# Both H transforms of the diagonal Fourier step as even and odd halves on 64x64 TensorE tiles, with GpSimd's additions and subtractions of rows 32 apart on either side

## The chip, the cores and the metric

One core of a Trainium2 chip runs the program; seven are idle. The metric is the device time of one execution in microseconds, the median of several runs.

## The reference

The input x has 8 images of 32 channels and 64x64 pixels. First comes one layer of content-dependent filtering (a 3x3 convolution to 16 channels, a leaky ReLU, a 1x1 convolution to nine logits, a softmax, and a 3x3 filter with these nine weights); the change leaves it alone. Then four layers of this, with h = 0.1:

```
Kj, Lj = project(K[j]), project(L[j])        # less their mean over the 3x3
z = relu(batchnorm(conv3x3(x, Kj)))
x = batchnorm(x + h * conv3x3T(z, Kj))
x = real(ifft2(fft2(x) * t)),  t = 1 / (h * |fft2(Lj)|^2 + 1)
```

batchnorm takes mean and variance over images and pixels, per channel. The last line is the Fourier step: a 2-d transform of every channel plane, a product with a real table, and the way back.

## The kernel before

**Layout.** An image pair (bp, four of them) has its channels and the row number modulo 4 on the 128 partitions, and 16 groups g of rows along the free side; X0 is the activation, Z0 the intermediate z, and X2, Z2 are the same moved by two rows, filled by DMA. A chunk c is a quarter of a pair, 4 groups, 512 columns, one PSUM bank; a layer has 16 chunks. All arithmetic is f32.

**Stages.** Per layer: `conv1` (16 chunks, 12 matmuls of 128x32 tiles each, into Z0), batchnorm and ReLU of z, `conv2` (16 chunks; VectorE adds 0.1 times each onto X0 at L864), the Fourier step per pair, and conv1 of the next layer. The Fourier step of a pair is a chain in which TensorE and VectorE take turns:

- `turn` (L879): VectorE transposes 32x32 blocks of X0 into one of three buffers `turned`.
- `fwdW` (L1113): 16 matmuls, the transform along W; VectorE transposes the four banks into `freqw` (L889).
- `slot0` and `fwdH` (L1123, L1129): the transform along H by one full 128x128 matmul a bank, four banks; VectorE multiplies with the table into `spec` (L912, L923). The frequency 0 of W holds two real columns and goes by itself: slot0, scaled, then slot0c (L1137), which ScalarE copies into `spec` (keep_slot0, L599).
- `invH` (L1146): the way back along H, a full matmul a bank; VectorE transposes into `backw` (L895).
- `invW` (L1160): 16 matmuls; VectorE transposes into `turned` again (move_back, L905), and ScalarE writes X0 from there with batchnorm's scale and bias (keep_invW, L614).

batchnorm's second use rides on the linearity of this: sums of X0 and of its square are taken by ScalarE behind each conv2 chunk (sum_x, L593), while the transform runs on unscaled data; the scale comes in at the end. Its chain is aggregate_x (L810 to L816), one small matmul (average, L1088), and scale_and_bias (L820 to L836). Behind it `prepare` (L657 to L665) makes the next layer's weights.

**What sets the order.** Each engine runs through the same list, layer_steps, and does its own part of each step, in that order. The eight PSUM banks are dealt out in the list's order: the step with number n has bank n % 8, and TensorE may start it once the last use of that bank has been read (Bank.claim). fwdW and invW start at a multiple of four. The buffers `turned` are used in rotation, 2 * bp + half modulo 3, on the way in and on the way back; move_back waits by x_back until the buffer's former content has been written to X0 (L904). SyncE copies X0 to X2 by DMA once half a pair is back (x_back), and conv1 waits for that.

## Time and profile before

| | |
|---|---|
| median of 3 runs | 695.63 us (694.91 to 696.49) |
| the profiled execution | 699.56 us, span 697.7 us |
| TensorE, matmuls | 643.2 us busy, 92% |
| VectorE | 487.7 us, 70% |
| ScalarE | 355.3 us, 51% |
| GpSimd | 95.5 us, 14% |
| TensorE's mean granted clock | 0.978 of full |

The span reaches from the first to the last instruction of the program; the execution's time has a little around it. The first 176 us are the filtering layer, in which GpSimd makes 80 of the products. A layer takes some 138 us behind it. The layers stand at 181.5, 319.0, 456.4 and 594.4 us (the first matmul of conv2). An engine's busy time is the union of its instructions; a matmul in f32 leaves two records, so that the counts of TensorE's rows are twice those of the code.

### The profile page before, as it was taken

The numbers are of one execution on the slowest core, as the hardware profiler recorded it, in microseconds if no ns is written. First come the engines' busy times: TensorE is split into PE (matmuls) and PEld (weight loads), VectorE is DVE, ScalarE is ACT, GpSimd is POOL, SyncE is SP. The second block draws the span as 40 slices with busy tenths as digits, with TensorE's granted clock in tenths as the row PEclk, the third lists the DMA queues.
The fourth block names the chain that finished last, engine by engine and source line by source line (L and its number), as shares of the span: only waits on it lengthen the run. The fifth ranks groups of instructions, "written<-read, shape, count | busy, mean of one in ns | idle before, by whom it ended". The sixth has DMA issues, their size and how long they took to land.

```text
span 697.7 us, 13525 instructions
## 1 busy us (share of the span) xinstructions
PE 643.2 (92%) x5392; PEld 221.3 (32%) x5392; DVE 487.7 (70%) x843; ACT 355.3 (51%) x672; POOL 95.5 (14%) x92
## 2 busy tenths in 40 slices
PE   6597999999999989999999899999998999999982
PEld 4222333222333333233333332333333323333330
DVE  3669888875886794638867946398679453886783
ACT  1454666663796223528961325299523152994233
POOL 0367666672000000000000000000000000000000
PEclk9689999999999999999999999999999999999996
DMA  9995111115800013583000226730003177100044
GB/s 187 183 171 91 32 32 33 31 31 127 190 2 1 1 28 97 131 176 102 1 1 1 52 72 156 155 99 1 1 1 79 46 176 154 40 1 1 1 105 137
DMA packets 44781, 51.10 MB, mean 73 GB/s; under 512 B 36528, under 2 KB 36656, under 8 KB 42672
## 3 DMA queue, kind: packets, MB, share of 16 engines
q1 hardware_dynamic: 40240, 48.95, 32.9%
q10 hardware_dynamic: 4480, 1.30, 1.2%
q8 instruction: 43, 0.70, 0.4%
q14 instruction: 18, 0.15, 0.1%
HBM read 11.96 MB, written 4.19 MB: 23 GB/s over the span
## 4 chain that ended last, share of the span: by engine, by line
PE 77%; DVE 15%; issue 3%; ACT 2%; DMA 1%; SPq 1%; POOL 0%; DVEq 0%; ACTq 0%; POOLq 0%
PE psum L978 48%; PE psum L1050 6%; PE psum L1146 5%; PE psum L1113 5%; PE psum L1129 3%; PE psum L1160 3%; PE psum L1001 3%; DVE work L923 2%; PE psum L1038 2%; DVE spare L895 1%; DVE work L889 1%; ACT Z L614 1%; DVE work L905 1%; DVE work L879 1%; PE psum L1080 1%
## 5 line engine op out<-in xcount | busy, mean ns | idle before, releaser
L978 PE MATMUL psum<-Z,wts 128*32 128x512 f32 x1536 | 168.2, 593 | 6.4 <-DVE Z L846 6.4
L978 PE MATMUL psum<-X,wts 128*32 128x512 f32 x1536 | 170.1, 593 | 0.6 <-issue 0.6
L593 ACT ACTIVATE work<-X,small 128x512 bf16<-128x512 f32 x128 | 90.7, 710 | 48.6 <-DVE X L864 48.6
L768 DVE BATCH_NORM_STATS2 stats<-Z 128x6 f32<-128x512 f32 x60 | 41.3, 692 | 79.3 <-ACT Z L508 79.2
L508 ACT ACTIVATE Z<-psum 128x512 f32<-128x512 f32 x64 | 38.2, 597 | 104.3 <-PE psum L978 93.2
L978 PEld LDWEIGHTS psum<-Z,wts 128*32 128x32 f32 x1536 | 51.6, 109 | 121.5 <-issue 108.5
L978 PEld LDWEIGHTS psum<-X,wts 128*32 128x32 f32 x1536 | 47.9, 109 | 111.7 <-issue 110.7
L571 ACT ACTIVATE Z<-Z,small 128x512 f32<-128x512 f32 (+4 forms) x92 | 80.2, 922 | 5.2 <-DVE small L836 4.7
L864 DVE SCALAR_TENSOR_TENSOR X<-psum,X 128x512 f32<-128x512 f32 x64 | 43.6, 690 | 39.0 <-PE psum L978 38.8
L1146 PE MATMUL psum<-work,cstS 128*128 128x512 f32 x128 | 59.2, 605 | 4.7 <-DVE work L889 3.9
L1129 PE MATMUL psum<-work,cstS 128*128 128x496 f32 x128 | 56.3, 582 | 0.0
L889 DVE STREAM_TRANSPOSE work<-psum 128x512 f32<-128x512 f32 x64 | 40.0, 680 | 16.6 <-PE psum L1113 16.6
L614 ACT ACTIVATE X<-work,small 128x512 f32<-128x512 f32 x36 | 28.7, 875 | 39.2 <-DVE work L905 39.2
L757 DVE TENSOR_TENSOR work<-Z,psum 128x512 f32<-128x512 f32 x52 | 33.6, 680 | 19.3 <-PE psum L1038 19.2
L923 DVE TENSOR_TENSOR work<-psum,tabT 128x496 f32<-128x496 f32 x64 | 39.6, 664 | 2.3 <-PE psum L1129 1.9
L1050 PE MATMUL psum<-work,cstS 128*32 128x512 f32 x168 | 36.2, 628 | 2.9 <-DVE spare L757 2.7
L1146 PEld LDWEIGHTS psum<-work,cstS 128*128 128x128 f32 x128 | 23.0, 189 | 40.6 <-issue 33.1
L757 DVE TENSOR_TENSOR spare<-Z,psum 128x512 f32<-128x512 f32 x48 | 30.9, 679 | 4.8 <-PE psum L1038 4.6
L1113 PE MATMUL psum<-work,cstS 32*64 32x512 f32 x384 | 31.4, 599 | 2.6 <-DVE work L923 2.6
L879 DVE STREAM_TRANSPOSE work<-X 128x512 f32<-128x512 f32 x48 | 32.1, 716 | 0.5
L905 DVE STREAM_TRANSPOSE work<-psum 128x1024 f32<-128x1024 f32 x24 | 28.8, 1225 | 5.1 <-PE psum L1160 5.1
L492 ACT ACTIVATE work<-psum 128x512 f32<-128x512 f32 x53 | 30.6, 595 | 2.9 <-ACT X L498 1.2
(122 smaller groups left out, 772.7 us busy)
## 6 DMA issues: line engine op xcount, KB each, us to landing
X<-X SPq DMA_DIRECT2D x64, 260.0 KB, 4.0
Z<-Z SPq DMA_DIRECT2D x32, 520.0 KB, 8.0
Z<-x SPq DMA_DIRECT2D x36, 128.0 KB, 4.2
out<-Z SPq DMA_DIRECT2D x24, 128.0 KB, 2.2
parS<-par SPq DMA_DIRECT2D x4, 673.0 KB, 8.6
Z<-x SPq DMA_DIRECT2D x12, 120.0 KB, 5.3
Z<-x ACTq DMA_DIRECT2D x14, 64.0 KB, 4.4
Z<-x SPq DMA_DIRECT2D x14, 64.0 KB, 4.7
```

The costliest lines, as they stand in the source:

```text
L571: last = nc.scalar.activation(z, z, ACT.Relu, bias=small[p0:p1, 13:14], scale=small[p0:p1, 12:13])
L593: nc.scalar.activation(by_row(rest[:, o:o + N // 2].bitcast(bf16)), xc, what, bias=small[:, 26:27], accum_out=sums[:, NCH * i + c:NCH * i ...
L757: nc.vector.tensor_tensor(by_line(product(c, dj, r)), around(c, dj, r), by_line(bank(n)), op=ALU.mult)\
L768: nc.vector.bn_stats(stats[:, 6 * c:6 * c + 6], rows(Z0, REG, c // Q, CH * (c % Q), CH))
L864: nc.vector.scalar_tensor_tensor(xc, in0=by_row(bank(n)), scalar=STEP, in1=xc, op0=ALU.mult, op1=ALU.add).then_inc(drained[n % BANKS], 1)
L889: nc.vector.transpose(freqw[:, N * q:N * q + N], src).then_inc(rows_moved, 1)
L923: nc.vector.tensor_tensor(to, src, tt, op=ALU.mult).then_inc(drained[n % BANKS], 1)
L978: last = nc.tensor.matmul(out_b[C * r:C * r + C, :], weights[:, o:o + C], rows(src, reg, bp, g, CH, dj - 1), start=(dj == 0), stop=(dj == ...
L1050: last = nc.tensor.matmul(bank(n)[C * r:C * r + C, :], cm(C_STACK, C), product(c, dj, r), start=(dj == 0), stop=(dj == 2), tile_position=( ...
L1113: last = nc.tensor.matmul(bank(first + r)[64 * half:64 * half + 64, :], cstS[k, C_FW + 64 * hi:C_FW + 64 * hi + 64], src[:, hi], start=(hi ...
L1129: nc.tensor.matmul(bank(n)[:, 0:16 * (SL - 1)], cm(C_FH), freqw[:, N * q:N * q + N].rearrange("p (a s) -> p a s", s=SL)[:, :, 1:SL], start ...
L1146: nc.tensor.matmul(bank(n), cm(to), spec[:, N * q:N * q + N], start=True, stop=True).then_inc(filled[n % BANKS], 1)
```

## The change

The transform along 64 rows splits by the parity of the frequency: even frequencies need only x[r] + x[r+32], odd ones only x[r] - x[r+32]. So the 128x128 matrix of H (real and imaginary part times 64 rows) falls into two of 64x64.

- GpSimd makes sums and differences of rows 32 apart (groups 8 apart) from X0 into Z0 (mix_halves), once conv2 has left both chunks. The turn takes both halves of a pair at once, from Z0, so it stands behind conv2's fifth chunk of a pair's count, and the Fourier steps move one chunk back in the list.
- fwdH and invH go by two banks: four matmuls of 64x64 at the four corners of the array, each bank half even, half odd. In the last layer invH remains a full matmul and puts the halves together itself. slot0, slot0c and the tables follow the new order of partitions.
- On the way back (not in the last layer) ScalarE scales the even and the odd buffer in place, the bias with the even one alone, and GpSimd writes their sum and difference into the two halves of X0 (unmix_halves). move_back's wait becomes one for the whole pair that had the buffer.
- ScalarE's sums are taken of Z0: the sum of the sums, and the squares of sums and differences, three instructions for two chunks instead of four; aggregate_x has two instructions more.
- In the list, aggregate_x moves behind fwdH of pair 2, scale_and_bias behind fwdW of pair 3, and invH of pair 3 ahead of the next conv1.

```diff
     after = {
-        5: fourier(j, 0, "fwdW"),
-        9: fourier(j, 0, "fwdH") + fourier(j, 1, "fwdW"),
-        13: fourier(j, 0, "invH") + fourier(j, 1, "fwdH") + fourier(j, 2, "fwdW"),
-        15: fourier(j, 1, "invH") + fourier(j, 2, "fwdH"),
+        6: fourier(j, 0, "fwdW"),
+        10: fourier(j, 0, "fwdH") + fourier(j, 1, "fwdW"),
+        14: fourier(j, 0, "invH") + fourier(j, 1, "fwdH") + fourier(j, 2, "fwdW"),
     }
     for c in range(NCH):
-        steps += [("conv2", j, c), ("turn", j, c)] + after.get(c, [])
-    steps += [("norm", j, 2)] + fourier(j, 3, "fwdW") + fourier(j, 0, "invW") + fourier(j, 2, "invH")
-    steps += fourier(j, 1, "invW") + fourier(j, 3, "fwdH")
-    rest = {1: fourier(j, 3, "invH"), 3: fourier(j, 2, "invW"), 5: fourier(j, 3, "invW")}
+        steps.append(("conv2", j, c))
+        if c and c % Q == 0:
+            steps.append(("turn", j, c // Q - 1))
+        steps += after.get(c, [])
+    steps += fourier(j, 1, "invH") + [("turn", j, BP - 1)] + fourier(j, 2, "fwdH") + fourier(j, 3, "fwdW")
+    steps += [("norm", j, 2)] + fourier(j, 0, "invW") + fourier(j, 2, "invH") + fourier(j, 1, "invW") + fourier(j, 3, "fwdH")
+    steps += fourier(j, 3, "invH")
+    rest = {3: fourier(j, 2, "invW"), 5: fourier(j, 3, "invW")}
     for c in range(NCH):
         if j + 1 < DEPTH:
             steps.append(("conv1", j + 1, c))
...
                     clear_edges(c // Q)
+
+            def mix_halves(j, bp, i):
+
+                bk.result(NUMBER["conv2", j, bp * Q + 2 + i])
+                low, high = (rows(X0, REG, bp, CH * (2 * half + i), CH) for half in range(2))
+                for half, op in enumerate((ALU.add, ALU.subtract)):
+                    nc.gpsimd.tensor_tensor(rows(Z0, REG, bp, CH * (2 * half + i), CH), low, high, op=op)\
+                        .then_inc(halves_mixed, 1)
+
+            def unmix_halves(j, bp):
+
+                pool.wait_ge(parts_scaled, 2 * (BP * j + bp) + 2)
+                even, odd = (turned[(2 * bp + p) % 3].rearrange("p (g b w) -> p g b w", b=2, w=W) for p in range(2))
+                for half, op in enumerate((ALU.add, ALU.subtract)):
+                    dst = rows(X0, REG, bp, 2 * CH * half, 2 * CH).rearrange("p g (w b) -> p g b w", b=2)
+                    nc.gpsimd.tensor_tensor(dst, even, odd, op=op).then_inc(x_back, 2)
+
+            for j in range(DEPTH):
+                for bp in range(BP):
+                    for i in range(2):
+                        mix_halves(j, bp, i)
+                for bp in range(BP if j + 1 < DEPTH else 0):
+                    unmix_halves(j, bp)
 
         @block.scalar
         def _(act):
...
-            def sum_x(j, c):
-                if c == 0:
+            def sum_x(j, bp):
+                if bp == 0:
                     act.wait_ge(shift_ready, j + 1)
-                bk.result(NUMBER["conv2", j, c])
-                xc = rows(X0, REG, c // Q, CH * (c % Q), CH)
-                for i, what in enumerate((ACT.Identity, ACT.Square)):
-                    m = 2 * (NCH * j + c) + i
-                    o = 4 * N - N // 2 * (m % 3 + 1)
-                    if m > 2:
-                        act.wait_ge(x_summed, m - 2)
-                    nc.scalar.activation(by_row(rest[:, o:o + N // 2].bitcast(bf16)), xc, what, bias=small[:, 26:27],
-                                         accum_out=sums[:, NCH * i + c:NCH * i + c + 1]).then_inc(x_summed, 1)
+                for i in range(2):
+                    act.wait_ge(halves_mixed, Q * (BP * j + bp) + 2 * i + 2)
+                    for s, (half, what) in enumerate(((0, ACT.Identity), (0, ACT.Square), (1, ACT.Square))):
+                        m = 3 * (2 * (BP * j + bp) + i) + s
+                        o = 4 * N - N // 2 * (s + 1)
+                        if m > 2:
+                            act.wait_ge(x_summed, m - 2)
+                        src = rows(Z0, REG, bp, CH * (2 * half + i), CH)
+                        bias = {} if half else {"bias": small[:, 26:27]}
+                        nc.scalar.activation(by_row(rest[:, o:o + N // 2].bitcast(bf16)), src, what, **bias,
+                                             accum_out=sums[:, PAIRS * s + 2 * bp + i:PAIRS * s + 2 * bp + i + 1])\
+                            .then_inc(x_summed, 1)
 
...
                 act.wait_ge(rows_back, 2 * (BP * j + bp) + q // 2 + 1)
+                if j < DEPTH - 1:
+                    if q % 2 == 0:
+                        part = turned[c // 2 % 3]
+                        bias = {} if q else {"bias": small[:, 13:14]}
+                        nc.scalar.activation(part, part, ACT.Identity, scale=small[:, 12:13], **bias).then_inc(parts_scaled, 1)
+                    return
                 src = turned[c // 2 % 3][:, N * (q % 2):N * (q % 2) + N].rearrange("p (g b w) -> p g b w", b=2, w=W)
-                if j == DEPTH - 1:
-                    both = Z2[:, bp * REG2:bp * REG2 + 2 * G * W].rearrange("p (b l w) -> p l b w", b=2, w=W)
-                    dst = both[:, CH * q:CH * q + CH]
-                else:
-                    dst = rows(X0, REG, bp, CH * q, CH).rearrange("p g (w b) -> p g b w", b=2)
+                both = Z2[:, bp * REG2:bp * REG2 + 2 * G * W].rearrange("p (b l w) -> p l b w", b=2, w=W)
+                dst = both[:, CH * q:CH * q + CH]
                 nc.scalar.activation(dst, src, ACT.Identity, bias=small[:, 13:14],
                                      scale=small[:, 12:13]).then_inc(x_back, 1)
 
...
-                src = X0[:, o + 2:o + 2 + g * GROUP].rearrange("p (g i) -> p g i", i=GROUP)[:, :, 0:ROW]
+                    nc.vector.tensor_scalar(S(26), stats[:, 1:2], -2.0, None, ALU.mult).then_inc(shift_ready, 1)
+
+            def turn(j, bp, half):
+
+                dve.wait_ge(halves_mixed, Q * (BP * j + bp) + 3 + half)
+                k, g = 2 * bp + half, 2 * CH
+                o = bp * REG + g * GROUP * half
+                src = Z0[:, o + 2:o + 2 + g * GROUP].rearrange("p (g i) -> p g i", i=GROUP)[:, :, 0:ROW]
                 for b in range(2):
                     dst = turned[k % 3].rearrange("p (m b c) -> p b m c", b=2, c=C)
                     last = nc.vector.transpose(dst[:, b], src.rearrange("p g (e l b) -> p b g e l", e=2, b=2)[:, b])
...
                 if k > 2:
-                    dve.wait_ge(x_back, NCH * j + 2 * (k - 2))
+                    dve.wait_ge(x_back, NCH * j + (2 * (k - 2) if j == DEPTH - 1 else Q * ((k - 3) // 2 + 1)))
                 nc.vector.transpose(turned[k % 3].rearrange("p (m e l) -> p e m l", e=2, l=32),
                                     psum[:, b0:b0 + 2, :].rearrange("p e (c m) -> p e m c", c=C)).then_inc(rows_back, 1)
 
...
-                            turn(*at)
+                        for half in range(2):
+                            turn(*at, half)
                     elif what == "fwdW":
                         move_rows(*at)
+                        if at[1] == 3 * Q + 3:
+                            scale_and_bias(j, 2)
                         if at[1] == 3 * Q + 3 and j + 1 < DEPTH:
                             dve.wait_ge(bn_ready, 2 * j + 2)
...
-                        if at[1] == 2 * Q - 1:
-                            aggregate_x(j)
                     elif what == "invW" and at[1] % 2 == 0:
                         move_back(j, at[1] // Q, at[1] % Q // 2)
                     elif what == "slot0":
@@ -956,7 +994,7 @@
                     elif what == "fwdH":
                         scale_fwdH(*at)
                         if at[1] == 2 * Q + 3:
-                            scale_and_bias(j, 2)
+                            aggregate_x(j)
                     elif what == "conv1":
                         conv1_stats(*at)
...
+                t = taps[:, N * (i % 2):N * (i % 2) + N]
+                nc.tensor.matmul(bank(n)[:, 0:N // 2], cm(e), t[:, 0:N // 2], start=True, stop=True)
+                for p in range(2):
+                    last = nc.tensor.matmul(bank(n)[64 - 64 * p:128 - 64 * p, N // 2:N], cstS[:, e + 64 * p:e + 64 * p + 64],
+                                            t[:, N // 2:N], start=True, stop=True, tile_position=(0, 64 - 64 * p))
+                last.then_inc(filled[n % BANKS], 1)
 
             def average(j, which):
...
             def forward_h(j, c):
-                n, q = NUMBER["fwdH", j, c], c % Q
-                bk.claim(n)
-                nc.tensor.matmul(bank(n)[:, 0:16 * (SL - 1)], cm(C_FH),
-                                 freqw[:, N * q:N * q + N].rearrange("p (a s) -> p a s", s=SL)[:, :, 1:SL],
-                                 start=True, stop=True).then_inc(filled[n % BANKS], 1)
+                first, q = NUMBER["fwdH", j, c], c % Q
+                for x in range(2):
+                    bk.claim(first + x)
+                for x in range(2):
+                    for p in range(2):
+                        k, half = slice(64 * p, 64 * p + 64), 64 * (p ^ x)
+                        src = freqw[k, N * (q + x):N * (q + x) + N].rearrange("p (a s) -> p a s", s=SL)[:, :, 1:SL]
+                        last = nc.tensor.matmul(bank(first + x)[half:half + 64, 0:16 * (SL - 1)], cstS[k, C_FH:C_FH + 64], src,
+                                                start=True, stop=True, tile_position=(64 * p, half))
+                    last.then_inc(filled[(first + x) % BANKS], 1)
...
             def inverse_h(j, c):
-                n, (bp, q) = NUMBER["invH", j, c], divmod(c, Q)
-                bk.claim(n)
-                bk.result(NUMBER["fwdH", j, c])
+                first, (bp, q) = NUMBER["invH", j, c], divmod(c, Q)
+                for x in range(2):
+                    bk.claim(first + x)
+                for x in range(2):
+                    bk.result(NUMBER["fwdH", j, c + x])
                 bk.result(NUMBER["slot0c", j, bp])
-                to = C_IL if j == DEPTH - 1 else C_IH
-                nc.tensor.matmul(bank(n), cm(to), spec[:, N * q:N * q + N], start=True,
-                                 stop=True).then_inc(filled[n % BANKS], 1)
+                for x in range(2):
+                    src = spec[:, N * (q + x):N * (q + x) + N]
+                    if j == DEPTH - 1:
+                        last = nc.tensor.matmul(bank(first + x), cm((C_IL, C_IX)[x]), src, start=True, stop=True)
+                    for p in range(2 if j < DEPTH - 1 else 0):
+                        k, half = slice(64 * (p ^ x), 64 * (p ^ x) + 64), slice(64 * p, 64 * p + 64)
+                        last = nc.tensor.matmul(bank(first + x)[half], cstS[k, C_IH + 64 * x:C_IH + 64 * x + 64], src[k],
+                                                start=True, stop=True, tile_position=(64 * (p ^ x), 64 * p))
+                    last.then_inc(filled[(first + x) % BANKS], 1)
```

Three places show what moves. The first is VectorE behind conv2's last chunk of a layer. Before (L864 the addition, L879 the turn, L895 invH, L811 to L816 the statistics, L912 and L923 the scaling, L889 fwdW):

```order
L864 SCALAR_TENSOR_TENSOR X<-psum,X 128x4x128 x2
L879 STREAM_TRANSPOSE work<-X 128x16x32 x2
L895 STREAM_TRANSPOSE spare<-psum 128x8x2x32 x4
L811 TENSOR_REDUCE small<-sums 128x2
L812 TENSOR_SCALAR small<-small 128x1
L813 TENSOR_SCALAR small<-small 128x2
L814 SCALAR_TENSOR_TENSOR small<-small 128x1
L815 TENSOR_SCALAR small<-small 128x1
L816 TENSOR_SCALAR small<-cstS,small 128x4
L912 TENSOR_TENSOR work<-psum,tabT 128x64
L923 TENSOR_TENSOR work<-psum,tabT 128x16x31 x4
```

And now (the same instructions are L902, L917, L933, L847 to L854, L950 and L961, L927):

```order
L902 SCALAR_TENSOR_TENSOR X<-psum,X 128x4x128
L933 STREAM_TRANSPOSE spare<-psum 128x8x2x32 x4
L917 STREAM_TRANSPOSE work<-Z 128x16x32 x4
L950 TENSOR_TENSOR work<-psum,tabT 128x64
L961 TENSOR_TENSOR work<-psum,tabT 128x16x31 x4
L847 TENSOR_REDUCE small<-sums 128x1
L848 TENSOR_REDUCE small<-sums 128x1
L849 TENSOR_SCALAR small<-small 128x1
L850 TENSOR_SCALAR small<-small 128x1
L851 TENSOR_SCALAR small<-small 128x1
L852 SCALAR_TENSOR_TENSOR small<-small 128x1
L853 SCALAR_TENSOR_TENSOR small<-small 128x1
```

The turn behind the last chunk has grown from two transposes to four, it stands behind those of invH, and the statistics have gone behind the scaling.

The second place is VectorE from the next layer's weights to conv1's statistics. Before (L905 move_back, L768 conv1's statistics):

```order
L657 TENSOR_REDUCE ksum<-parS 128x64
L665 SCALAR_TENSOR_TENSOR wts<-ksum,cstS,parS 128x96 x4
L670 COPY small<-parS 128x2
L905 STREAM_TRANSPOSE work<-psum 128x2x16x32 x2
L895 STREAM_TRANSPOSE work<-psum 128x8x2x32 x4
L905 STREAM_TRANSPOSE third<-psum 128x2x16x32
L905 STREAM_TRANSPOSE work<-psum 128x2x16x32
L912 TENSOR_TENSOR work<-psum,tabT 128x64
L923 TENSOR_TENSOR work<-psum,tabT 128x16x31 x4
L768 BN_STATS stats<-Z 128x6 x2
L895 STREAM_TRANSPOSE spare<-psum 128x8x2x32 x4
```

And now (move_back is L943, conv1's statistics L804):

```order
L943 STREAM_TRANSPOSE work<-psum 128x2x16x32 x2
L933 STREAM_TRANSPOSE work<-psum 128x8x2x32 x4
L943 STREAM_TRANSPOSE third<-psum 128x2x16x32
L943 STREAM_TRANSPOSE work<-psum 128x2x16x32
L950 TENSOR_TENSOR work<-psum,tabT 128x64
L961 TENSOR_TENSOR work<-psum,tabT 128x16x31 x4
L933 STREAM_TRANSPOSE spare<-psum 128x8x2x32 x4
L804 BN_STATS stats<-Z 128x6 x4
```

The order is the same but for invH of pair 3, which now stands ahead of conv1. The second of the two single move_backs (pair 1, second half) is the one that now waits for GpSimd's whole unmix of pair 0.

The third place is TensorE behind conv2's last chunk, up to conv1. Before:

```order
L1146 MATMUL psum<-work,cstS 128x512 x4
L1123 MATMUL psum<-work,cstS 128x64
L1129 MATMUL psum<-work,cstS 128x496 x4
L1137 MATMUL psum<-work,cstS 128x64
L1088 MATMUL psum<-small,cstS 128x5
L1113 MATMUL psum<-work,cstS 64x512 x16
L1160 MATMUL psum<-work,cstS 32x512 x16
L1146 MATMUL psum<-work,cstS 128x512 x4
L1160 MATMUL psum<-spare,cstS 32x512 x16
L1123 MATMUL psum<-work,cstS 128x64
L1129 MATMUL psum<-work,cstS 128x496 x4
L1137 MATMUL psum<-work,cstS 128x64
```

And now (invH is L1212, slot0 L1170 and L1172, fwdH L1184, slot0c L1195, fwdW L1155, the small matmul L1130, invW L1227, conv1 L1016), from invW of pair 0 on:

```order
L1227 MATMUL psum<-work,cstS 32x512 x16
L1212 MATMUL psum<-work,cstS 64x512 x8
L1227 MATMUL psum<-spare,cstS 32x512 x16
L1170 MATMUL psum<-work,cstS 128x2x16
L1172 MATMUL psum<-work,cstS 64x2x16 x2
L1184 MATMUL psum<-work,cstS 64x496 x8
L1195 MATMUL psum<-work,cstS 64x2x16 x4
L1212 MATMUL psum<-work,cstS 64x512 x8
L1016 MATMUL psum<-X,wts 32x512 x48
```

Four full matmuls have become eight of 64x64, and the last invH stands ahead of conv1's first chunk instead of behind its second.

## Rows read from the trace of the kernel before

**Rows 1.** The page, part 1: busy time and share of the span.
```profile
PE 643.2 (92%) x5392; PEld 221.3 (32%) x5392; DVE 487.7 (70%) x843; ACT 355.3 (51%) x672; POOL 95.5 (14%) x92
```
**Rows 2.** Busy time by stretch: conv2, the tail, conv1 (layer 2).
```profile
core 0: us, PE busy (x) PEld busy (x) DVE busy (x) ACT busy (x) POOL busy (x), PEclk, DMA share, GB/s
456.40:515.40 59.00, 58.82 (x513) 20.32 (x513) 44.99 (x67) 42.58 (x87) 0.00 (x0) 1.00 0.07 20
515.40:539.60 24.20, 21.01 (x142) 9.01 (x138) 22.85 (x51) 8.25 (x15) 0.00 (x0) 1.00 0.20 47
539.60:588.90 49.30, 49.27 (x457) 14.88 (x457) 21.76 (x30) 15.24 (x25) 0.00 (x0) 1.00 0.57 130
```
**Rows 3.** Order of time on PE in layer 0: start us, us, engine, line.
```profile
209.52 0.47 PE L1123 MATMUL psum<-work,cstS 128*128 128x64 f32 x2
...
215.59 10.51 PE L978 MATMUL psum<-Z,wts 128*32 128x512 f32 x96
226.04 3.70 PE L1146 MATMUL psum<-work,cstS 128*128 128x512 f32 x8
229.57 0.38 PE L1123 MATMUL psum<-work,cstS 128*128 128x64 f32 x2
229.78 3.50 PE L1129 MATMUL psum<-work,cstS 128*128 128x496 f32 x8
233.12 0.33 PE L1137 MATMUL psum<-work,cstS 128*128 128x64 f32 x2
233.38 0.66 PE L1113 MATMUL psum<-work,cstS 32*64 32x512 f32 x4
...
235.29 5.36 PE L978 MATMUL psum<-Z,wts 128*32 128x512 f32 x48
```
**Rows 4.** Order of time behind conv2 in layer 2, and one window of it.
```profile
515.39 3.70 PE L1146 MATMUL psum<-work,cstS 128*128 128x512 f32 x8
...
516.25 1.31 DVE L879 STREAM_TRANSPOSE work<-X 128x512 f32<-128x512 f32 x2
...
520.98 2.40 DVE L923 TENSOR_TENSOR work<-psum,tabT 128x496 f32<-128x496 f32 x4
...
525.91 2.51 DVE L889 STREAM_TRANSPOSE work<-psum 128x512 f32<-128x512 f32 x4 [0.69 <-PE psum L1113]
...
530.48 2.38 DVE L905 STREAM_TRANSPOSE work<-psum 128x1024 f32<-128x1024 f32 x2
...
539.63 5.36 PE L978 MATMUL psum<-X,wts 128*32 128x512 f32 x48 [0.60 <-issue]
...
523.30:525.21 1.91, 1.58 (x32) 0.69 (x32) 1.57 (x11) 0.29 (x1) 0.00 (x0) 1.00 0.00 0
```
**Rows 5.** GpSimd's products in the prologue: duration ns min/median/max.
```profile
L446 POOL TENSOR_TENSOR work<-Z,work x21: 1172/1183/1448, 29.5 to 158.2; 128x512 f32<-128x512 f32 x21
```
**Rows 6.** ScalarE's instructions by shape: busy us, mean ns.
```profile
L571 ACT ACTIVATE Z<-Z,small 128x1024 f32<-128x1024 f32 x4 | 4.9, 1228 | 0.0
```
**Rows 7.** The tail of layer 1, same columns as rows 2.
```profile
378.00:401.60 23.60, 20.94 (x143) 9.02 (x139) 22.22 (x50) 7.65 (x14) 0.00 (x0) 1.00 0.18 45
```
**Rows 8.** DMA issues: KB each, median us to landing.
```profile
X<-X SPq DMA_DIRECT2D x64, 260.0 KB, 4.0
```
**Rows 9.** TensorE at rest and at work, and the granted clock (PEclk).
```profile
21.30 1.99 PE L1015 MATMUL psum<-w2S,work 128*128 128x72 f32 x8 [2.94 <-ACT work L462]
...
682.14 1.92 PE L1160 MATMUL psum<-spare,cstS 64*32 64x512 f32 x32
...
21.00:22.00 1.00, 0.70 (x3) 0.70 (x4) 0.00 (x0) 0.25 (x1) 0.00 (x0) 0.66 1.41 172
33.00:38.00 5.00, 5.00 (x24) 0.91 (x16) 2.79 (x6) 1.08 (x3) 0.17 (x1) 0.50 1.05 165
38.00:39.00 1.00, 1.00 (x16) 0.30 (x16) 0.39 (x1) 0.66 (x1) 0.72 (x1) 0.81 0.97 167
686.50:687.00 0.50, 0.00 (x0) 0.00 (x0) 0.50 (x1) 0.50 (x2) 0.00 (x0) 0.91 0.00 0
```

78 lines of the change are left out of this document (49 added, 29 removed).

## Prediction

> **What bounds the kernel now.** I read the page first: TensorE (PE) is busy for 92% of the span, VectorE (DVE) for 70%, GpSimd (POOL) for 14%, all of that in the prologue [rows 1]. A share is an average, so the stretches of a layer come next [rows 2]. In the stretch of conv2, PE is busy 58.82 us of 59.00 and DVE 44.99. From conv2's end to the next conv1, PE is busy 21.01 of 24.20 us and DVE 22.85. In conv1's stretch PE is busy 49.27 of 49.30. The clock is full in all three. So PE sets the pace except in the 24 us behind conv2 (I call them the tail), where DVE does. What follows is a sum over these stretches, layer by layer.
>
> **What TensorE gives up.** Four banks by full 128x128 tiles take 3.5 us of issue: invH runs from 226.04 to slot0 at 229.57, fwdH from 229.78 to slot0c at 233.12 [rows 3]. Tiles in different rows and columns of the array run beside each other already: the sixteen 32x64 matmuls of fwdW take 235.29 - 233.38 = 1.91 us for four banks [rows 3]. So four 64x64 tiles should fill two banks in the time of one: for four banks fwdH 3.34 -> 1.7 us, invH 3.53 -> 1.75. PE saves 1.65 us in each of 16 fwdH and 1.8 us in each of 12 invH (the last layer's stay full tiles), 48 us in all. The question is how much of it reaches the end.
>
> The Trainium skill (TensorEngine Tiling (Array Packing), Theoretical Speedup) gives up to 2x for a dimension of 64 or less. By it the 48 us would come off whole, which makes 648 us. The rows of the tail speak against it.
>
> **What DVE allows.** DVE reads every one of those banks, and its price stays: four scalings of fwdH 2.40 us, four transposes of fwdW 2.51 (invH's are alike), two of invW 2.38, two of the turn 1.31 [rows 4]. That is 0.6 us a bank against PE's new 0.43. And fwdW claims the four banks that slot0 and the first three of fwdH had, so PE waits for DVE's third scaling. Behind conv2 chunk 10 (now chunk 9): slot0 0.25 us, the first pair full at 1.3, DVE's third scaling done at 3.15, fwdW issued 3.35 to 5.3; before, 215.59 - 209.52 = 6.07 [rows 3]. Saved: 0.8. Behind chunk 14 (now 13): invH 1.75, DVE's four transposes 1.1 to 3.6, its scalings of slot0 and three banks to 5.6, fwdW 5.8 to 7.7; before, 235.29 - 226.04 = 9.25 [rows 3]. Saved: 1.55. In the last layer, with full invH, the second is 0.45.
>
> **What GpSimd adds.** mix_halves has the form of the prologue's products, 128x512 f32 from two SBUF operands, median 1.18 us [rows 5]. Per pair of images there are four, the last two started by conv2's fourth chunk and done 2.4 us later. The turn stands behind the next chunk's addition, 2.6 us later, so in the middle of a layer nobody waits. unmix_halves does two of 1024 elements, with an output in steps of two. No row shows that size. It can hardly be cheaper than one of 512, 1.18, nor dearer than twice the slowest one, 2 x 1.45 = 2.9 [rows 5]. I take 2.3, near twice the median.
>
> **The tail, step by step,** from t = 0, where PE is through with conv2 chunk 15 (515.39 in the rows). Now [rows 4]: addition, two transposes of the turn at 0.9, four of invH, statistics, scalings to 8.0, fwdW's transposes 10.5 to 13.0, weights to 15.1, invW's transposes to 17.5, conv1 at 24.2. DVE works almost without a gap.
> New: addition to 0.85; GpSimd's last mix 0.9 to 3.25; meanwhile invH 1's transposes 1.1 to 3.55 on DVE, then the turn, now four transposes (of both halves, since rows 32 apart come together only here), to 6.05; slot0 and four scalings to 8.55; aggregate_x, two instructions longer, to 9.8. PE has issued invH 1 and fwdH 2 by 3.65 and can issue fwdW 3 only behind the turn and the second scaling, at 7.6. fwdW's transposes run 9.9 to 12.4, scale and bias (1.9 us, a window of its own in the rows) to 14.25, weights to 16.4, move_back of pair 0 to 18.85: 1.35 us later than the 17.5 of now.
> Then the new wait. move_back of pair 1's second half writes the buffer of pair 0's first half, and now waits for the whole unmix of pair 0. ScalarE scales 1024 elements in place (1.23 us, the row of that size [rows 6]) twice, to 20.2, GpSimd twice 2.3, to 24.9. DVE is there at 22.4 and stands 2.5 us. Behind it in DVE's queue are the scalings of fwdH 3, to 28.7; on ScalarE keep_slot0 stands behind pair 1's scaling, 27.8. invH 3, now ahead of conv1, ends at 29.7, and conv1 starts at 29.8. Before, conv1 started at 24.2 (layer 2) or 23.6 (layers 0 and 1 [rows 7]) and gave 3.55 us to invH 3 later. Like for like, that is 27.8 and 27.1. The tail costs 2.0 in layer 2 and 2.7 in the others. The copy to X2 (4.0 us to landing [rows 8]) starts at 22.6 and is in time.
>
> **conv1's stretch.** Pairs 2 and 3 leave through ScalarE and GpSimd too. conv1 chunk 8 stands at t = 54.6; its input is unmixed at 48.6 and copied at 53.2. Chunk 12 has more room. Nothing is added; but the cover is 1.4 us, and a GpSimd slower by more would open it.
>
> **Sum at full clock.** Layers 0 and 1: -0.8 - 1.55 + 2.7 = +0.35 each. Layer 2: -0.35. Layer 3 has no unmix; its two places save 0.8 and 0.45, and its chain reaches invW 2 at 28.8 instead of 27.0 (longer turn, late fwdW), +1.8: +0.55. In all +0.9 us. At no cost: ScalarE's sums (96 instead of 128, off the chain), the tables (half of a bank as two tiles side by side, the same passes), the wider constants (loaded under the prologue's work).
>
> **The clock.** The walk opens idle stretches on PE that the kernel now lacks: 3.65 to 7.6 and 23.5 to 27.9, each with only slot0c's four tiny matmuls inside, besides two of about 3 us. In the prologue PE stood 2.94 us until 21.30, and in that microsecond the granted clock fell from 1.00; at the end PE stops at 684.06 and it falls at about 686.95 [rows 9]. So 2.9 us of rest sufficed twice. It came back at about 38.4, after PE had been busy for all of 33.0 to 38.0 at 0.50 [rows 9]: 5.4 us at half pace lose 2.7. A fall in the late gap costs about that; a fall in the early one also lengthens fwdW and invW on the chain by 1.9 each, in all about 6.5.
> The Trainium skill (TensorE: Matmul & The Clock Gate, HAM oscillation) warns of just such gaps between bursts. With it the sum is 701.9, without it 696.5. The rows decide for it: both gaps are longer than the two that brought the clock down.
> I take two falls of 2.7 over the tails, +5.4.
>
> **Numbers.** The profiled execution is 699.56 us with a span of 697.7; the median of the runs is 695.63, 3.9 lower. I put the change on the median: 695.63 + 0.9 + 5.4 = 701.9.
>
> **Rivals.**
> 1. The clock stays up: 696.5, give or take 1.5. For it: the slot0c matmuls inside both gaps. Against: the length of the gaps. Chance 0.13.
> 2. Faster: PE's gain comes out whole in conv2's stretch. It decides at fwdW's claim: if DVE's third scaling is done when PE arrives, the two places save 1.65 and 3.45 instead of 0.8 and 1.55, 2.75 more per layer, and 2.1 more in the last: 0.9 - 8.3 - 2.1 = -9.5, which makes 686.1. Half of that, with my walk too long by 1 us a tail, gives 688. For it: DVE has 14 idle us in that stretch [rows 2]. Against: they lie elsewhere than in these bursts. This is what is left of the 2x rule, whose whole I hold for below 0.02. Chance 0.27, with times from 684 to 694.
> 3. GpSimd is slower on the strided output. At the upper bound of 2.9, DVE's stand grows by 1.2 us in three tails, 705.5; if the steps doubled its time to 4.6, by 4.6 and more, since conv1's cover goes as well, 716. Chance 0.10.
> 4. The change doesn't do what it says: the 64x64 tiles run two by two, with nothing saved on PE. The two places keep their length and the tail adds the same: 704 to 709. Against: the fwdW row. Chance 0.05.
> The forecast has 0.45, from 698 to 709.
>
> About 0.2%, 1.4 us, is what a measurement of this kernel can tell from no change. Faster by more: 0.27. Within: 0.12 (most of rival 1). Slower by more: 0.61. The range 687 to 712 leaves out the far ends of rivals 2 and 3.
>
> **What would show it.** In the new profile: fwdH and invH of four banks at 1.7 us on PE; conv2's stretch near 56.7 us; conv1's start near 30 us behind conv2's end; the second move_back of pair 1 waiting for GpSimd some 2.5 us; GpSimd 2.3 us for 1024 elements; a granted clock below 1.00 in some of the tails. I am wrong if conv2's stretch falls below 55 us, if conv1 starts within 28 us, or if the clock never leaves 1.00 in a layer.

## The result, and the profile after

The changed kernel took 713.44 us (median of 4 runs, 711.72 to 717.23) against 696.06 for the kernel before on the same chip (694.91 to 696.96): ratio 1.0258, 95% interval 1.0214 to 1.0302. It is 17 us slower, and 1.4 us beyond the upper end of the predicted range. The profiled execution took 713.42 us, with a span of 711.6 us; the mean granted clock went from 0.978 to 0.949.

The page after, busy time and the granted clock in 40 slices; the first answers to [rows 1]:

```profile
PE 627.1 (88%) x5840; PEld 205.7 (29%) x5840; DVE 494.9 (70%) x851; ACT 319.4 (45%) x584; POOL 232.8 (33%) x180
...
PEclk9699999999999988999999889999987999999996
```

TensorE (PE) was busy 16 us less, not 48: part of its work ran at half clock, and slot0 and the tables got dearer (below). The clock row shows where the clock fell: at the ends of layers 0, 1 and 2. The last layer has one short fall as well (676.7 to 680.2), too short for a digit; the 6 at the end stands behind the last matmul. By stretch in layer 2, with the columns of [rows 2]:

```profile
464.80:521.65 56.85, 54.78 (x560) 18.49 (x561) 42.99 (x65) 35.28 (x69) 17.65 (x14) 1.00 0.06 18
521.65:553.60 31.95, 22.86 (x210) 7.20 (x207) 26.28 (x58) 7.55 (x13) 10.81 (x6) 0.79 0.14 36
553.60:599.20 45.60, 45.60 (x452) 12.99 (x450) 22.68 (x27) 13.47 (x19) 10.58 (x5) 1.00 0.59 137
```

conv2's stretch is 2.15 us shorter. The tail is 7.75 longer, and 3.7 of that comes back in conv1's stretch, which no longer holds invH of pair 3. In the tail the granted clock is 0.79 where it was 1.00.

PE in conv2's stretch of layer 0, which answers to [rows 3] (slot0 L1170, fwdH L1184, conv2 L1016, invH L1212):

```profile
212.58 0.42 PE L1170 MATMUL psum<-work,cstS 128*128 128x32 f32 x2
...
218.17 10.51 PE L1016 MATMUL psum<-Z,wts 128*32 128x512 f32 x96
228.61 1.95 PE L1212 MATMUL psum<-work,cstS 64*64 64x512 f32 x16
230.49 0.41 PE L1170 MATMUL psum<-work,cstS 128*128 128x32 f32 x2
...
231.08 1.90 PE L1184 MATMUL psum<-work,cstS 64*64 64x496 f32 x16
232.79 0.37 PE L1195 MATMUL psum<-work,cstS 64*64 64x32 f32 x8
```

invH of four banks takes 230.49 - 228.61 = 1.88 us (it was 3.53), fwdH 232.79 - 231.08 = 1.71 (3.34). slot0, now in three pieces, takes 231.08 - 230.49 = 0.59 where it took 0.21 [rows 3]. The group behind chunk 10 takes 218.17 - 212.58 = 5.59.

The tail of layer 0 on PE answers to the PE rows of [rows 4]. t = 0 is 238.86, where PE is through with chunk 15; in brackets the idle time before and what ended it:

```profile
238.86 1.95 PE L1212 MATMUL psum<-work,cstS 64*64 64x512 f32 x16
...
245.12 0.42 PE L1195 MATMUL psum<-work,cstS 64*64 64x32 f32 x8 [1.90 <-DVE work L950]
246.28 3.43 PE L1155 MATMUL psum<-work,cstS 32*64 32x512 f32 x32 [0.74 <-DVE work L961]
...
253.14 3.41 PE L1227 MATMUL psum<-work,cstS 64*32 64x512 f32 x32 [2.92 <-DVE work L927]
...
266.96 0.51 PE L1195 MATMUL psum<-work,cstS 64*64 64x32 f32 x8 [2.85 <-DVE work L950]
268.26 3.69 PE L1212 MATMUL psum<-work,cstS 64*64 64x512 f32 x16 [0.79 <-ACT work L631]
271.88 3.36 PE L1016 MATMUL psum<-X,wts 128*32 128x512 f32 x20
```

Three groups run at half clock: fwdW 3 (3.43 us where 1.98 is normal), invW 0 (3.41 for 1.95) and invH 3 (3.69 for 1.88, with conv1's first chunk behind it). Each stands behind a gap. conv1 starts at t = 33.0; before, at 23.6 in this layer.

The wait that I had announced, on VectorE (DVE), and the GpSimd (POOL) instructions that it waited for:

```profile
261.64 1.25 DVE L943 STREAM_TRANSPOSE third<-psum 128x1024 f32<-128x1024 f32 x1
265.45 1.25 DVE L943 STREAM_TRANSPOSE work<-psum 128x1024 f32<-128x1024 f32 x1 [2.56 <-POOL X L471]
```

```profile
260.62 4.70 POOL L471 TENSOR_TENSOR X<-work 128x1024 f32<-128x1024 f32 x2 [18.33 <-ACT work L644]
```

And from the groups of the page (idle before them at the end):

```profile
L462 POOL TENSOR_TENSOR Z<-X 128x512 f32<-128x512 f32 x64 | 80.7, 1285 | 251.0 <-DVE X L902 251.0
...
L471 POOL TENSOR_TENSOR X<-work 128x1024 f32<-128x1024 f32 x12 | 28.3, 2383 | 60.7 <-ACT work L644 60.7
```

Last, a stretch that I had booked at nothing: from conv1's end to conv2. Before, and after (the tables are L1080, then L1119 and L1121):

```profile
175.94 1.98 PE L1080 MATMUL psum<-work,cstS 128*128 128x512 f32 x4
...
181.57 1.92 PE L978 MATMUL psum<-Z,wts 128*32 128x512 f32 x16 [1.58 <-DVE Z L846]
```

```profile
175.83 0.70 PE L1119 MATMUL psum<-work,cstS 128*128 128x256 f32 x2
176.46 0.65 PE L1121 MATMUL psum<-work,cstS 128*64 128x256 f32 x4
177.04 0.70 PE L1119 MATMUL psum<-work,cstS 128*128 128x256 f32 x2
...
182.05 1.50 PE L1016 MATMUL psum<-Z,wts 128*32 128x512 f32 x12 [1.08 <-DVE Z L884]
```

A table of two pieces now takes 177.04 - 175.83 = 1.21 us where it took about 0.95, and the stretch is 6.22 us long instead of 5.63. The four tables cost 1.04 us more; PE's wait ahead of conv2, 1.08 instead of 1.58, takes back 0.5 of it, and 0.6 is left.

**The span's balance** (711.6 - 697.7 = +13.9): tables 4 x 0.6 = +2.4; conv2's stretches -2.2 three times and -0.75 in the last; tail and conv1 together +6.6, +4.5, +4.1, and from conv2's end to the end of layer 3 +3.8, which is +19.0; the part ahead of the tables of layer 0 -0.1.

The medians lie 17.4 apart, 3.5 more than the two spans: the profiled execution of the kernel before is 3.5 us above its median, the one of the change is on it. What the layers' rows show of the change is 14 us; where the rest stands, no row shows. The part ahead of the first conv1, which the change leaves alone, takes up to 4 us more or less from one execution to another (last section), so below, a difference of medians stands beside what the profiles show from the first conv1 on.

### The profile page after: what moved, and what is told of

It is laid out like the page before. It is cut to its first block, busy times and chain, and to the rows that moved or that the text cites. A ratio compares the mean times of both kernels' runs of the same rounds, so it can differ in the third digit from the quotient of the medians.

```text
span 711.6 us, 14466 instructions
## 1 busy us (share of the span) xinstructions
PE 627.1 (88%) x5840; PEld 205.7 (29%) x5840; DVE 494.9 (70%) x851; ACT 319.4 (45%) x584; POOL 232.8 (33%) x180
## 4 chain that ended last, share of the span: by engine, by line
PE 72%; DVE 16%; ACT 4%; issue 3%; POOL 2%; DMA 1%; SPq 1%; DVEq 0%; ACTq 0%; POOLq 0%
PE psum L1016 46%; PE psum L1088 6%; PE psum L1155 5%; DVE work L961 3%; PE psum L1227 3%; PE psum L1039 3%; PE psum L1212 2%; PE psum L1209 2%; POOL X L471 2%; PE psum L1076 2%; DVE work L927 1%; DVE work L917 1%; ACT work L644 1%; ACT Z L649 1%; DVE work L943 1%
## 5 line engine op out<-in xcount | busy, mean ns | idle before, releaser
L1016 PE MATMUL psum<-Z,wts 128*32 128x512 f32 x1536 | 168.2, 593 | 4.3 <-DVE Z L884 4.3
L1016 PE MATMUL psum<-X,wts 128*32 128x512 f32 x1536 | 171.2, 598 | 0.1
L462 POOL TENSOR_TENSOR Z<-X 128x512 f32<-128x512 f32 x64 | 80.7, 1285 | 251.0 <-DVE X L902 251.0
L804 DVE BATCH_NORM_STATS2 stats<-Z 128x6 f32<-128x512 f32 x60 | 40.9, 691 | 68.4 <-ACT Z L537 68.0
L1016 PEld LDWEIGHTS psum<-Z,wts 128*32 128x32 f32 x1536 | 52.4, 109 | 117.1 <-issue 108.9
L1016 PEld LDWEIGHTS psum<-X,wts 128*32 128x32 f32 x1536 | 47.4, 110 | 117.9 <-issue 116.6
L624 ACT ACTIVATE work<-Z,small 128x512 bf16<-128x512 f32 x64 | 45.5, 712 | 53.9 <-POOL Z L462 53.9
L902 DVE SCALAR_TENSOR_TENSOR X<-psum,X 128x512 f32<-128x512 f32 x64 | 43.3, 676 | 36.1 <-PE psum L1016 36.0
L927 DVE STREAM_TRANSPOSE work<-psum 128x512 f32<-128x512 f32 x64 | 39.9, 683 | 18.2 <-PE psum L1155 18.2
L471 POOL TENSOR_TENSOR X<-work 128x1024 f32<-128x1024 f32 x12 | 28.3, 2383 | 60.7 <-ACT work L644 60.7
L961 DVE TENSOR_TENSOR work<-psum,tabT 128x496 f32<-128x496 f32 x64 | 38.5, 659 | 3.3 <-PE psum L1184 3.3
L943 DVE STREAM_TRANSPOSE work<-psum 128x1024 f32<-128x1024 f32 x24 | 29.3, 1236 | 15.5 <-POOL X L471 8.3
L1155 PE MATMUL psum<-work,cstS 32*64 32x512 f32 x384 | 33.7, 651 | 7.2 <-DVE work L961 7.2
L644 ACT ACTIVATE work<-work,small 128x1024 f32<-128x1024 f32 x18 | 21.2, 1193 | 38.6 <-DVE work L943 38.6
L452 POOL TENSOR_TENSOR tabT<-Z,work 128x512 f32<-128x512 f32 x21 | 24.7, 1189 | 26.6 <-PE psum L1088 26.6
L1212 PE MATMUL psum<-work,cstS 64*64 64x512 f32 x192 | 29.4, 735 | 2.3 <-ACT work L631 2.3
```

Source lines behind the costliest of these rows:

```text
L462: nc.gpsimd.tensor_tensor(rows(Z0, REG, bp, CH * (2 * half + i), CH), low, high, op=op)\
L471: nc.gpsimd.tensor_tensor(dst, even, odd, op=op).then_inc(x_back, 2)
L624: nc.scalar.activation(by_row(rest[:, o:o + N // 2].bitcast(bf16)), src, what, **bias, accum_out=sums[:, PAIRS * s + 2 * bp + i:PAIRS * s ...
L902: nc.vector.scalar_tensor_tensor(xc, in0=by_row(bank(n)), scalar=STEP, in1=xc, op0=ALU.mult, op1=ALU.add).then_inc(drained[n % BANKS], 1)
L927: nc.vector.transpose(freqw[:, N * q:N * q + N], src).then_inc(rows_moved, 1)
L961: nc.vector.tensor_tensor(to, src, tt, op=ALU.mult).then_inc(drained[n % BANKS], 1)
```

## The experiments

Three costs are candidates in the tail: the clock, DVE's wait for GpSimd, and the new place of invH 3. Each was taken away alone. Differences are to the median of the kernel before in the same series (696.59 us for the clock alone, DVE's wait alone, the place of invH 3 and the tables alone; 697.26 for the last two below; 697.10 for the other four; 19 to 23 runs each); the change itself stands at +17.4.

**The clock alone.** Full-size matmuls whose result nobody reads fill PE's gaps in the tail. The order of the work stays.

```diff
+            def filler(n, cols):
+                for m in cols:
+                    nc.tensor.matmul(bank(n)[:, 0:m], cm(C_AVG), cstS[:, 0:m], start=True, stop=True)
 ...
+                if bp == 2:
+                    filler(n, (512, 512) if j < DEPTH - 1 else (512,))
+                if bp == 3 and j < DEPTH - 1:
+                    filler(n, (512, 512, 512))
```

(with 512, 512 and 256 columns ahead of invW 0, and 256 ahead of invH 3, 512 in the last layer.)

> The changed kernel with full-size filler matmuls (their results are overwritten) on TensorE wherever it stands in a tail: 2 of 512 columns ahead of slot0c of pair 2, 2.5 ahead of invW of pair 0, 3 ahead of slot0c of pair 3, half a one ahead of invH of pair 3. By my theory the granted clock is half of what the tails cost: conv1 and the last transforms run at half pace after each gap, 9.7 us over the four tails beyond the walk at full clock. Then the clock stays at 1.00 in all layers and the time falls from 713.4 to 704, give or take 1.5. Rival: VectorE's queue and GpSimd alone make the tails long, and the low clock falls where TensorE waits anyway: 712 to 715 with the clock up.

Measured: 704.02 us (703.17 to 704.63), ratio 1.0101 (1.0065 to 1.0137), clock 0.975: +7.4. The tail of layer 0 on PE (t = 0 at 236.93; L1190 is the filler):

```profile
244.36 1.98 PE L1155 MATMUL psum<-work,cstS 32*64 32x512 f32 x32 [0.80 <-DVE work L961]
...
256.23 3.51 PE L1240 MATMUL psum<-spare,cstS 64*32 64x512 f32 x32 [2.60 <-DVE work L943]
...
266.06 1.95 PE L1222 MATMUL psum<-work,cstS 64*64 64x512 f32 x16
267.94 2.35 PE L1016 MATMUL psum<-X,wts 128*32 128x512 f32 x20
```

fwdW 3 and invH 3 are back at full clock, and conv1 starts at t = 31.0 instead of 33.0. The clock still falls once, ahead of invW 1 (3.51 us), here and in layer 1 (3.06). In layer 2 (t = 0 at 515.14) the same gap brings no fall, and conv1 starts at t = 29.8:

```profile
534.08 1.95 PE L1240 MATMUL psum<-spare,cstS 64*32 64x512 f32 x32 [2.58 <-DVE work L943]
...
544.95 10.52 PE L1016 MATMUL psum<-X,wts 128*32 128x512 f32 x96
```

By the medians the fillers give back 17.4 - 7.4 = 10.0 us. The two profiles, from the first conv1 to the end, give 8.3: 3.0, 1.5 and 2.3 from conv2's end to the next conv2, and 1.5 in the last layer. So the clock is 8 to 10 us of the cost.

**DVE's wait alone.** A fourth buffer for pair 1's second half, in the part of Z2 that is free then, so that move_back need not wait for pair 0's unmixing. No filler.

```diff
+        o4 = 3 * REG2 + GROUP
+        fourth = Z2[:, o4:o4 + 2 * N]
+
+        def back(j, k):
+            return fourth if k == 3 and j < DEPTH - 1 else turned[k % 3]
 ...
-                if k > 2:
+                if k > 2 and (j == DEPTH - 1 or k != 3):
```

> The changed kernel with a fourth buffer (free columns of Z2 of pair 3) for the second half of pair 1 on the way back, so that VectorE's move_back no longer waits for GpSimd's unmix of pair 0. Theory: this stand of 2.5 us is on the chain in three tails, so 7.5 us go, 706, and up to 5 more if the shorter gap keeps the clock up (701). Rival: the next wait ends at the same time (keep_slot0 behind ScalarE's scaling, or conv1 on the copy to X2), and the time stays above 711.

Measured: 699.93 us (698.0 to 704.07), ratio 1.0046 (1.0016 to 1.0076), clock 0.953: +3.3. Its tail in layer 0 (t = 0 at 238.99):

```profile
246.42 3.48 PE L1160 MATMUL psum<-work,cstS 32*64 32x512 f32 x32 [0.74 <-DVE work L966]
...
253.32 3.50 PE L1232 MATMUL psum<-work,cstS 64*32 64x512 f32 x32 [2.96 <-DVE work L932]
...
264.47 0.42 PE L1200 MATMUL psum<-work,cstS 64*64 64x32 f32 x8 [0.18 <-DVE work L955]
265.77 2.22 PE L1217 MATMUL psum<-work,cstS 64*64 64x512 f32 x16 [0.88 <-ACT work L636]
267.92 6.65 PE L1021 MATMUL psum<-X,wts 128*32 128x512 f32 x60
```

The gap ahead of slot0c is 0.18 us instead of 2.85, invH 3 is fast again, and conv1 starts at t = 28.9. The early falls (fwdW 3, invW 0) are unchanged. By the medians one buffer took away 14 us, more than I had allowed for: DVE's wait and the clock fall behind it. In the profiles the three layers that the edit touches are 5.1, 3.3 and 3.1 us shorter, 11.5 in all, and the last layer, which it leaves alone, is 1.9 longer: the clock fell there at other places.

**Both.** The buffer, and of the fillers only the early ones.

> The fourth place for pair 1's second half (699.9 us alone) and, beside it, full-size filler matmuls on TensorE in the two early gaps of each tail: two of 512 columns ahead of slot0c of pair 2, and 512, 512 and 256 columns ahead of invW of pair 0. Theory (the stand and the clock are two separate costs, and with the fourth place only the two early falls are left, each of which makes one group of about 1.9 us take 3.4 to 3.5): at most 2 falls x 1.5 us x 3 layers plus about 1 in the last layer would come off if TensorE were the path there, but part of it lies beside VectorE's chain, so 694 to 697 us, granted clock 0.97 or more. Rival (the groups behind the early falls wait for VectorE and ScalarE anyway): 699 to 700.5, with the clock up and the time the same. Second rival (fillers delay the groups behind them): above 701.

Measured: 696.72 us (694.79 to 697.70, 12 runs), ratio 0.9993 (0.9975 to 1.001), clock 0.976: level with before. Layer 0 (t = 0 at 234.99) and, below, invH 3 of the last layer:

```profile
242.42 1.98 PE L1160 MATMUL psum<-work,cstS 32*64 32x512 f32 x32 [0.81 <-DVE work L966]
...
254.28 3.38 PE L1241 MATMUL psum<-spare,cstS 64*32 64x512 f32 x32 [2.59 <-DVE work L948]
...
263.92 10.52 PE L1021 MATMUL psum<-X,wts 128*32 128x512 f32 x96
...
672.25 3.67 PE L1220 MATMUL psum<-work,cstS 128*128 128x512 f32 x8 [1.46 <-ACT work L636]
```

```profile
679.40 5.37 PE L1214 MATMUL psum<-work,cstS 128*128 128x512 f32 x8 [1.47 <-ACT work L636]
```

(the last row is that invH with the buffer alone.) It stands at -0.4. With the early fillers in both, the buffer is worth 7.4 + 0.4 = 7.8 us by the medians, 2.6 a tail, near DVE's wait of 2.56; by the profiles conv1 starts 2.1, 3.2 and 1.0 us sooner. With the buffer in both, the early fillers are worth 3.3 + 0.4 = 3.7 by the medians and 4.9 by the profiles. Of the 10.0 of the clock some 6 would then be left for the late gap, but that is a subtraction: no run fills the late gap alone.

Most of the early fillers' worth stands in the last layer, 3.3 us (from conv2's end to the span's end, 50.0 us without fillers and 46.7 with them), since PE and its full invH are the chain there. (The change, with the same instructions in that layer, took 48.1: it had one fall there instead of two.) In layer 0 they gain nothing: conv1 starts at t = 28.9 with them and without, since now the clock falls in a gap of 2.59 us that DVE opens ahead of invW 1. Layer 1 of the same run (t = 0 at 372.33) has the same gap and no fall, and conv1 starts at t = 27.2, so this fall costs 1.8 us:

```profile
391.30 1.95 PE L1241 MATMUL psum<-spare,cstS 64*32 64x512 f32 x32 [2.60 <-DVE work L948]
...
399.49 10.52 PE L1021 MATMUL psum<-X,wts 128*32 128x512 f32 x96
```

**The place of invH 3 alone**, in the changed kernel:

```diff
-    steps += fourier(j, 3, "invH")
-    rest = {3: fourier(j, 2, "invW"), 5: fourier(j, 3, "invW")}
+    rest = {1: fourier(j, 3, "invH"), 3: fourier(j, 2, "invW"), 5: fourier(j, 3, "invW")}
```

> The changed kernel with invH of pair 3 back behind the second chunk of conv1. Theory: conv1 stands behind VectorE's scaling of pair 3 only because of this place; it starts about 4.4 us earlier and gives 1.9 us later to invH: 2.5 us in each of three tails, 706, and less time at half clock, down to 702. Rival: conv1's first chunk then waits for the copy of pair 0 to X2, which is late through GpSimd, and the time stays at 712 or above.

Measured: 709.84 us (707.59 to 714.13), ratio 1.0193 (1.0142 to 1.0244): +13.3, which is 4.1 less than the change where at least 7 had been expected. With four runs each the ranges overlap (the change: 711.72 to 717.23), so that even the 4.1 is not firm.

```profile
267.37 0.64 PE L1194 MATMUL psum<-work,cstS 64*64 64x32 f32 x8 [2.86 <-DVE work L949]
267.94 8.20 PE L1015 MATMUL psum<-X,wts 128*32 128x512 f32 x48
```

In layer 0 conv1 starts 4.1 us sooner (t = 28.9) and does its first two chunks at half clock, 8.20 us where 5.36 is normal. The half clock fell on invH 3 in the change; here it falls on conv1, and the layer is 0.2 us shorter. In layer 1 the clock stayed up behind a gap of 2.86 us, and the layer is 2.3 shorter: the place is worth what I expected of it only where the clock does not fall.

**The tables alone**, put into the kernel before: half of each bank as two tiles of 64 columns.

```diff
-                nc.tensor.matmul(bank(n), cm(e), taps[:, N * (i % 2):N * (i % 2) + N], start=True,
-                                 stop=True).then_inc(filled[n % BANKS], 1)
+                t = taps[:, N * (i % 2):N * (i % 2) + N]
+                nc.tensor.matmul(bank(n)[:, 0:N // 2], cm(e), t[:, 0:N // 2], start=True, stop=True)
+                for p in range(2):
+                    last = nc.tensor.matmul(bank(n)[64 * p:64 + 64 * p, N // 2:N], cstS[:, e + 64 * p:e + 64 * p + 64],
+                                            t[:, N // 2:N], start=True, stop=True, tile_position=(0, 64 * p))
+                last.then_inc(filled[n % BANKS], 1)
```

> The kernel before with only the tables changed: half of each bank by one full tile, the other half by two tiles of 64 columns side by side, as in the changed kernel. In the new trace conv2 starts 6.2 us behind the end of conv1, before 5.6 us. Theory: each change between tile shapes costs about 0.15 us, the four tables 0.6 us a layer, 2.4 us in all: ratio 1.003. Rival: nothing (the six tenths came from GpSimd or the clock): ratio 1.000.

Measured: 699.0 us (697.46 to 699.33, 10 runs), ratio 1.0021 (1.0001 to 1.0041): +2.4, just clear of nothing, and +1.9 by the profiles. The layers are 138.1, 138.1 and 137.9 us apart, 137.4, 137.4 and 138.0 before.

**The forward half alone.** The inverse H is a full product again, ScalarE writes X0 itself, and there is no unmixing, hence no wait for GpSimd; once with invH 3 ahead of conv1, once behind its second chunk.

```diff
-            unmix_halves(j, bp)
 ...
-                    for p in range(2 if j < DEPTH - 1 else 0):
-                        k, half = slice(64 * (p ^ x), 64 * (p ^ x) + 64), slice(64 * p, 64 * p + 64)
 ...
+                    to = (C_IL, C_IX) if j == DEPTH - 1 else (C_IH, C_JX)
+                    last = nc.tensor.matmul(bank(first + x), cm(to[x]), src, start=True, stop=True)
```

> Forward H as halves only: the inverse H is the full 128x128 product of the kernel before again in every layer, ScalarE writes the layer's input directly, and GpSimd has no unmixing; mixing, forward halves, tables' tiles and the order of the tail stay as changed. Theory (the unmixing behind the inverse makes VectorE stand and costs 2.5 us a tail, the inverse as halves gives back 0.8 us at chunk 10, and the early clock falls come from TensorE being too fast ahead of VectorE in the tail, on the forward side): the stand and its fall go (like the fourth place, -13.5), the invH groups take 3.5 instead of 1.8 us (two on the path of a tail at the most, +2 to +5 in all): 702 to 706. Rival (the inverse side makes the early gaps too, and its full groups fill them): 698 or less. Second rival (the halves' forward side alone is what costs): 710 or more.

Measured: 720.78 us median, but of four runs from 709.29 (mean clock 0.973) to 722.14 (0.954), so that no ratio is given. Even the fastest lies above the 706 that I expected: a miss.

> The same with invH of pair 3 issued behind conv1's first chunk, where the kernel before has it. Theory: the full-size invH of pair 3 (3.5 us) leaves the path to conv1 and comes back as cover, so 2 to 5 us below the run with the forward halves only: about 699, still above the kernel before (696.6) by the tables' 2.4. Rival (its place is worth nothing with the stand gone, since the order of work on TensorE is only exchanged): the same as that run within 1 us.

Measured: 707.82 us (704.94 to 709.81), ratio 1.0148 (1.0115 to 1.0181): +10.7, a miss by 9. Layer 0, t = 0 at 237.93:

```profile
251.62 2.81 PE L1218 MATMUL psum<-work,cstS 64*32 64x512 f32 x32 [2.90 <-DVE small L856]
254.37 4.49 PE L1204 MATMUL psum<-work,cstS 128*128 128x512 f32 x8
```

I had thought that nearly all of the loss stands behind the inverse. But the forward side alone, with no wait for GpSimd anywhere, loses 10.7: tail and conv1 take 2.4, 3.7 and 1.4 us more than before in layers 0 to 2. Part of it is in these rows: the gap of 2.90 us ahead of invW 0 and the half clock behind it (invW 2.81, invH 4.49 where 1.95 and 3.70 are normal, 1.6 us). Its conv2 stretch is 0.7 shorter per layer, and its tables cost what the change's do. Where the rest of the tail's loss comes from was not taken apart.

**A version that beats both.** To the buffer and the early fillers, the tables' second halves as one full tile again, from a second, swapped copy of the constants:

```diff
-                for p in range(2):
-                    last = nc.tensor.matmul(bank(n)[64 - 64 * p:128 - 64 * p, N // 2:N], cstS[:, e + 64 * p:e + 64 * p + 64],
-                                            t[:, N // 2:N], start=True, stop=True, tile_position=(0, 64 - 64 * p))
+                last = nc.tensor.matmul(bank(n)[:, N // 2:N], cm(C_SW + 128 * (i // 2)), t[:, N // 2:N], start=True, stop=True)
 ...
+    c[:, C_SW:C_SW + 256] = tables[:, :, np.roll(by_parity, 64)].reshape(128, 256)
```

> The same as the run with the fourth place and the early fillers, and the tables' second halves as one full tile each again, with a constant whose column halves are swapped beside the present one. Theory (two tiles of 64 columns with a change of tile shape cost 0.6 us per layer in the change, 0.6 to 0.9 in the kernel before with the tables' tiles alone): 2.4 to 3 us less than that run, 692 to 694, which would be below the kernel before (696.6). Rival (the stretch of the tables is bounded by ScalarE's copies or by the wait ahead, and the tiles only looked dear): less than 1 us less.

Measured: 694.31 us (691.76 to 696.67, 12 runs), ratio 0.9951 (0.993 to 0.9972): 2.4 below the run with the tiles, as expected, and 2.8 below the kernel before (1.7 by the profiles).

```profile
174.18 0.70 PE L1125 MATMUL psum<-work,cstS 128*128 128x256 f32 x2
174.72 0.59 PE L1126 MATMUL psum<-work,cstS 128*128 128x256 f32 x2
175.15 0.59 PE L1125 MATMUL psum<-work,cstS 128*128 128x256 f32 x2
```

A table takes 175.15 - 174.18 = 0.97 us. The same without any filler:

> The fourth place and the full tables' tiles, without any filler. Theory (costs add up: the change 713.4, the stand with the fall it brings -13.5, the tables -2.4): 697 to 698, level with the kernel before within 0.3%; the fillers then are worth 3 us, and with them the halves beat the kernel before. Rival (the fillers do nothing for the time and the last run owes its 694.3 to the tables alone): 694 to 695.

Measured: 699.42 us (697.43 to 700.79, 11 runs), ratio 1.0022 (1.0005 to 1.0039), clock 0.955: +2.2, 1.1 below the buffer alone instead of 2.4, and 5.0 above the run with fillers; a miss by 1.4. The rival falls: the fillers are needed. By the profiles they are worth 3.8: 5.0 in the last layer and 0.3 and 0.2 in layers 2 and 1, while layer 0 with them was 1.5 longer, for the fall ahead of invW 1.

And with fillers, full tables and invH 3 behind conv1's second chunk:

> The run with the fourth place, the early fillers and the full tables' tiles (694.3 us), with invH of pair 3 issued behind conv1's first chunk instead of ahead of it, as the kernel before has it. In that run's profile invH of pair 3 waits 0.9 us for ScalarE and takes 2.2 us ahead of conv1, at full clock. Theory (TensorE is the path from there on, and conv1 needs nothing of pair 3 in its first chunks): conv1 starts 3.1 us earlier at full clock and has 1.9 us more in it, so 1.2 us less for each of three tails, 3.5 us in all: 690 to 692. Rival (the place is worth nothing: GpSimd's unmixing of pair 3, now 3 us later, is late for conv1's last chunks, or the clock falls at conv1's start as it did with invH behind alone): 694 or more.

Measured: 696.3 us (694.36 to 701.76, 12 runs), ratio 0.9996 (0.9973 to 1.0018): no gain, a miss. In layer 0 conv1 starts at t = 27.2 (of 234.24), 1.8 sooner than in the run above it with fillers, and gives 1.9 back to invH 3. What holds it (GpSimd, then PE, then the queue that copies X0's rows to X2):

```profile
254.62 4.69 POOL L476 TENSOR_TENSOR X<-work 128x1024 f32<-128x1024 f32 x2 [16.96 <-ACT work L649]
```

```profile
261.44 5.36 PE L1021 MATMUL psum<-X,wts 128*32 128x512 f32 x48 [1.55 <-issue]
```

```profile
259.34 0.46 SPq L382 DMA_DIRECT2D X<-X  x1
259.84 0.60 SPq L383 DMA_DIRECT2D X<-X  x1
```

GpSimd is through with pair 0 at 259.31, the copies are issued at 259.34 and 259.84, and conv1 starts 2.1 us behind the first, after standing 1.55 us. That conv1 waited for these copies is read from the order of the rows, not tested.

## Why the prediction was wrong, by its own steps

- **What TensorE gives up:** right. invH takes 1.88 us, predicted as 1.75, fwdH 1.71 for 1.7, and 64x64 tiles run four at a time; rival 4 (two by two) is out.
- **What DVE allows:** right, and with it rival 2 is out. Behind chunk 10, 5.59 us for 5.3; behind chunk 14, 236.15 - 228.61 = 7.54 for 7.7; conv2's stretch 56.85 for 56.7. In the last layer 0.75 is saved for 1.25.
- **What GpSimd adds:** right. 1.285 us for 1.18, and 2.38 for 2.3; rival 3 is out.
- **The tail, step by step:** the mechanism was right, with its size at full clock. DVE stands 2.56 us for 2.5, fwdW 3 starts at t = 7.4 for 7.6. conv1 was to start at t = 29.8. It started at 33.0, 31.2 and 32.0 in the three tails, with the fillers at 31.0, 30.4 and 29.8, and the last is the one of the three in which the clock stayed up throughout. Before, the tails of layers 0 and 1 were alike, so the spread comes with the falls.
- **Sum at full clock, "the tables at no cost":** wrong, a term put at nothing for the count of passes alone. The passes are the same, but each table took 0.26 us more, of which 0.6 a layer reached the end, 2.4 in all. The run on the tables alone (+2.4, interval from 0.1) and the one with full tables (2.4 less) show it.
- **The clock, "two falls of 2.7 over the tails, +5.4":** this step failed. I knew that 2.9 us of rest had sufficed twice and saw two long gaps, but I counted falls as if most tails would be spared, and left out the two gaps "of about 3 us". Every tail had falls: three, two, two and one, with 41 us at half clock in all, and layer 0's came in gaps of 1.90 and 0.74, 2.92 and 2.85 us. The fillers priced them at 8.3 (profiles) to 10.0 us (medians). So the count was far too low, two for eight, and the price of one too high, 2.7 us for 1.0 to 1.3. With one fall in each of four tails at my own 2.7, 10.8 in all, the text would have had 707.3, by two errors that cancel in part.
- **The sum:** 0.9 + 5.4 = 6.3 us was to be added. The profiles, from the first conv1 on, have 14.1: 2.9 more of clock, 2.3 of tables, 1.5 in the tails beside the clock's 8.3 (0.9, 0.3, -0.2, 0.4; the first two have the fall that the fillers left) and 1.0 less saved in conv2's stretches. On the base of 695.63 that gives 709.7, inside the range; the medians have 713.0. The last 3.3 us are in no row, and their cause stays open.
- **The range:** its upper end, 712, held a slower GpSimd, but no case with a clock fall in every tail. The sign (0.61 for slower) and rival 1's fall (the clock does leave 1.00) came out as argued.

The Trainium skill (TensorE: Matmul & The Clock Gate, HAM oscillation) had warned of gaps between bursts. I weighed it as a yes or no. The trace agrees: every tail had a fall behind such a gap. But not every gap brought one (2.85 us ahead of slot0c in layer 2 of the run with the place of invH 3 moved did, 2.86 in layer 1 did not).

## What to carry to other kernels

An engine that isn't waited for gains nothing by being faster, and TensorE can lose: 48 us less of matmul opened gaps of 1.9 to 2.9 us in a stretch that VectorE paced, and half clock behind them cost 8 to 10 us. Where a change thins TensorE's work, count the gaps that it opens, and book a likely clock fall for every one like these, in every pass of the loop. Before a restructured transform is judged, take its side costs away one by one: here one buffer (14 us by the medians, with the fall it brought), fillers in two gaps (4 us) and undivided tables (2.4 us) turn 713.4 us into 694.3. Compare profiles stretch by stretch too: a stretch that no edit touched can differ by 2 to 4 us.

## What was not expected of the hardware

- Shorter gaps than the two of [rows 9] came ahead of a fall: 2.59 and 2.60 us ahead of invW 1 (3.38 and 3.51 us for 1.95). The same gap does not always bring a fall: 2.58 us in layer 2 and 2.60 in layer 1 of the same two runs left the clock at 1.00, and conv1 started 1.2 and 1.8 us sooner than in layer 0.
- Filling one gap moved the fall to the next: with the early gaps full, the one ahead of invW 1, which the buffer alone had at 0.94 us, was 2.59, and the clock fell there in two layers of three.
- 128x64 tiles side by side between 128x128 ones are not free: 1.21 us for a table, 0.97 with full tiles.
- The part ahead of conv1 of the first layer, which no edit touched, took from 69.0 us (the last run above) to 73.3 us (the profile of the kernel before) from one execution to another. It may be part of why that profile lies above the median; no trace of a faster execution of that kernel shows it. The clock goes with it: the profile of the kernel before has it at half until about 38.4 us [rows 9], the run with buffer and early fillers (first conv1 at 69.2 us) until 35.4, and from 36 to 38 us it is at full there:

```profile
36.00:38.00 2.00, 2.00 (x24) 0.52 (x20) 1.01 (x2) 1.14 (x2) 1.20 (x2) 1.00 1.00 172
```

Why it came back sooner is not shown.
